# Two layers of attention and experts: first loads, first maxima, score order and expert weights moved

## The chip, the cores and the metric

The kernel runs on one core of a Trainium2 chip. The metric is the device time of one execution in microseconds (us). Three runs of the kernel before gave 2292.01, 2292.16 and 2296.86 us; the median is 2292.16 us.

## What is computed

Two transformer layers on x of shape (2, 1024, 128), all in float32, each with a layer norm ahead of it:

```python
x = x + _L0_attn_ref(_layernorm(x), ...)   # 16 heads of 8, rotary embedding, plain softmax attention
x = x + _L0_ffn_ref(_layernorm(x), ...)    # one shared and 7 routed experts of width 352, top 2, silu gate
x = x + _L1_attn_ref(_layernorm(x), ...)   # layer norm with gain, biases, plain attention, residual inside
x = x + _L1_ffn_ref(_layernorm(x), ...)    # below
```

The last of them has an attention with relative positions and 32 experts of width 128:

```python
q, k, v = x @ wq, x @ wk, x @ wv                        # 16 heads of 8
p = pe @ wp                                             # pe: sines and cosines of 2*1024-1 distances
ac = jnp.einsum('bihd,bjhd->bhij', q, k)
bd_full = jnp.einsum('bihd,phd->bhip', q, p)
bd = bd_full[:, :, jnp.arange(Ss)[:, None], rel]        # rel = i - j + Ss - 1
att = jax.nn.softmax((ac + bd) * scale, axis=-1)
src = src + attn_out @ wo
x2 = _layernorm(src, ln2_g, ln2_b)
sel = jax.nn.sigmoid(x2 @ sel_w)                        # top 4 of 32 kept as gate
h = jax.nn.relu(jnp.einsum('bsd,edh->bseh', x2, keys))
moe_out = jnp.einsum('bseh,ehd,bse->bsd', h, values, gate)
```

## The kernel before

The program is written for each engine by hand: every engine has its own list of steps, in the order of `plan`, and counts semaphores. The ten stages are `front(0)`, `attention(0)`, `front(1)`, `experts0`, `front(2)` (with the end of `experts0` ahead of it), `attention(1)`, `front(3)`, `relative_attention`, `front(4)`, `experts1`. The engines meet only after stages 3, 4, 9 and 10 (`MEETINGS`); elsewhere each runs on as far as its semaphores let it. In the profile, SP is the queue that issues every DMA, PE is TensorE, DVE VectorE, ACT ScalarE, POOL GpSimd.

**Fronts** (f = 0, 2, 3 lead to an attention). The tokens go through in four groups g of 512. For each group the layer norm is taken, transposed and multiplied with the weights; ACT rounds keys and queries to a high part (`projected`, lines 1293 to 1310, tile `hl`), DVE or POOL subtracts to get the low part, and SP stores both to `q_stack` and `k_stack` in DRAM (`q_out` line 322, `k_out` line 332: three DMAs of 256 KB each). There is one `hl`: ACT may write group g + 1 only when the stores of group g have landed (`stk_out`, `stq_out`). Groups 0 and 1 are batch 0, and so heads 0 to 15. In the third group (g = 2) SP waits for the stores of groups 0 and 1 and issues the loads of heads 0, 1 and 2 (`load_qk`, line 358: four DMAs of 128 KB for queries and four for keys of each head; `load_rel` adds one of 32 KB, line 363). In fronts 0 and 2 they stand between `q_out` and `k_out` of the third group, in front 3 behind both.

**Plain attention** (`attention`, stages 2 and 6, 32 heads each). The work of one head is a `position` with eight steps kt. In each step PE issues `turned` twice (T below, line 607: one matmul each, keys by queries turned, on rows 0 to 63 of the array, into banks 0, 1, 7), `scores` of the head two ahead (S below, line 587: two matmuls on rows 64 to 127, into banks 2, 3 or 4, 5) and `values` (line 617). DVE takes the maximum of each S (`row_max`, line 1114), ACT the exponential of each T (line 1373). T waits for an exponential that frees its bank, S for a maximum that frees its pair. The maxima go as a row into the head's queries (`max_row`, `max_copy`, `max_rows`), so T has the maximum subtracted. S of heads 0 and 1 are made ahead of the first position.

**Relative attention** (stage 8). The same scheme; a head's positions are prepared by four `prep` (PE line 676 into bank 7, DVE line 1130, POOL lines 1604 and 1606, ACT line 1402), and each S is two `stack_scores` (line 685) and two `scores` (line 693) into banks 2 and 3, one pair only:

```python
e.wait_ge(max_done, 2 + 8 * (HB + n) + qt)
```

so that each S waits for the maximum (DVE line 1135) of the S just before it. T uses banks 0, 1, 4 and 5 (`TURN`). The S of heads 0 and 1 are made ahead of the first position, in four halves of four rows, each half after two `prep`.

**Last experts** (`experts1`, stage 10). For each of 32 experts x and four groups tg: PE multiplies keys (three matmuls of split operands, into bank tg), DVE gates (lines 1226, 1228), ACT rounds high (line 1491), POOL (tg 0, 1; line 1668) or DVE (tg 2, 3; line 1214) subtracts, PE multiplies values. PE's order is keys(x, tg), then values of the group before. The weights of an expert are split too: ACT rounds them (line 1498), POOL subtracts (line 1662) into `wsp`, which has four slots; POOL does so behind its two subtractions of the expert before, and keys(x, 0) waits for it (`wsp_ok`).

## Time and profile before

| | |
|---|---|
| the three runs, median | 2292.16 us |
| the profiled execution, its own time | 2293.8 us |
| its span, first to last instruction | 2291.8 us |
| PE busy | 2071.1 us (90%) |
| DVE busy | 1418.5 us (62%) |
| ACT busy | 1191.4 us (52%) |
| POOL busy | 518.3 us (23%) |
| mean granted TensorE clock | 0.927 of 2.4 GHz |
| line 1114, maxima of the plain attentions | 512, mean 1220 ns |
| line 1373, their exponentials | 1024, mean 589 ns |
| line 1135, maxima of the relative attention | 256, mean 1225 ns |
| line 1668, POOL's subtractions in the last stage | 64, mean 1292 ns |

A span holds everything from the first to the last instruction of the profiled execution; the execution's own time is 2.0 us longer. Matmuls are pipelined and their ends are modelled, so PE's busy share says little alone. A timeline gives instructions in order of time with the idle time before them and what ended it; the windows view gives busy time, granted clock and DMA traffic in stretches. PEclk 0.5 is 1.2 GHz, 1.0 is 2.4 GHz.

### The profile page before, as it was taken

To read this page: it belongs to the slowest core of one execution; us is meant where nothing else is said; L and a number is where in the kernel's file an instruction comes from. 1 tells how busy PE (TensorE), PEld (TensorE's weight loads), DVE (VectorE), ACT (ScalarE), POOL (GpSimd) and SP (SyncE) were. 2 spreads that over 40 slices of the span, in tenths; PEclk is the share of its full clock that TensorE was granted. 3 is DMA by queue.
4 is the path that set the end of the run, shared out by engine and by line. 5 is a ranking of instruction groups with operands and counts; after the bars stand their busy time and mean duration, and the time that the engine had idled before them with its cause. 6 is when DMAs were issued, how large, how long until landed. Compare 5 with 4: busy or idle time off the path is not lost.

```text
span 2291.8 us, 42807 instructions
## 1 busy us (share of the span) xinstructions
PE 2071.1 (90%) x13696; PEld 1163.3 (51%) x13696; DVE 1418.5 (62%) x1857; ACT 1191.4 (52%) x2289; POOL 518.3 (23%) x497
## 2 busy tenths in 40 slices
PE   5799999689984999999559999999999999976998
PEld 2244444367762344444325555555555555544776
DVE  4799999456655999996644444444444444335666
ACT  1488888456651688888203444444444444433443
POOL 1000000258861000000121221122212221013554
PEclk8599999789996799999758999999999999988999
DMA  7444453222105344442440112111221112013554
GB/s 235 110 107 123 105 124 87 68 80 85 46 0 151 99 120 108 124 105 78 136 108 22 44 48 59 43 43 43 58 48 43 43 45 62 8 49 126 205 189 158
DMA packets 94607, 202.48 MB, mean 88 GB/s; under 512 B 20368, under 2 KB 53648, under 8 KB 89104
## 3 DMA queue, kind: packets, MB, share of 16 engines
q1 hardware_dynamic: 94544, 201.69, 31.3%
q8 instruction: 33, 0.54, 0.1%
q14 instruction: 30, 0.25, 0.0%
HBM read 166.62 MB, written 36.57 MB: 89 GB/s over the span
## 4 chain that ended last, share of the span: by engine, by line
PE 38%; issue 5%; POOL 3%; DVE 3%; DMA 1%; SPq 1%; ACT 0%; POOLq 0%; DVEq 0%; ACTq 0%
PE PS L708 15%; PE PS L693 8%; PE PS L718 6%; PE PS L702 5%; POOL BIG_r L1668 2%; PE PS L676 2%; POOL PR_r L1662 1%; PE PS L781 1%; DVE M L1135 1%; PE PS L685 1%; SPq L358 0%; DMA Ws_r<-w_stack 0%; PE PS L726 0%; DMA rope<-r_dram 0%; DVE rt L1130 0%
## 5 line engine op out<-in xcount | busy, mean ns | idle before, releaser
L1114 DVE TENSOR_REDUCE M<-PS 128x1 f32<-128x1024 f32 x512 | 606.3, 1220 | 75.5 <-PE PS L587 71.4
L1373 ACT ACTIVATE PR<-PS 128x512 f32<-128x512 f32 x1024 | 535.2, 589 | 127.4 <-PE PS L607 126.7
L1135 DVE TENSOR_REDUCE M<-PS 128x1 f32<-128x1024 f32 x256 | 313.5, 1225 | 438.0 <-PE PS L693 438.0
L1410 ACT ACTIVATE PR<-PS 128x512 f32<-128x512 f32 x512 | 305.1, 597 | 463.3 <-PE PS L708 456.7
L607 PE MATMUL PS<-Qs_r,Ks_r 32*128 32x512 f32 x1024 | 371.2, 507 | 1.8 <-ACT PR L1373 1.4
L617 PE MATMUL PS<-PR,Va 128*32 128x256 f32 x4096 | 322.0, 399 | 0.0
L587 PE MATMUL PS<-Ks_r,Qs_r 32*128 32x512 f32 x1024 | 269.4, 521 | 43.3 <-DVE hl L1036 17.3
L607 PEld LDWEIGHTS PS<-Qs_r,Ks_r 32*128 32x128 f32 x1024 | 152.5, 186 | 251.1 <-ACT PR L1373 177.8
L1540 POOL TENSOR_TENSOR Va<-Vt,nil 128x64 f32<-128x64 f32 x96 | 27.7, 292 | 759.5 <-PE PS L617 627.7
L1604 POOL TENSOR_TENSOR qk<-rt 128x512 f32<-128x512 f32 x64 | 81.9, 1280 | 381.2 <-DVE rt L1130 381.2
L718 PE MATMUL PS<-PR,Va 128*32 128x256 f32 x2048 | 163.6, 391 | 0.1
L708 PE MATMUL PS<-BIG_r,Eh 128*128 128x512 f32 x512 | 159.3, 392 | 0.0
L617 PEld LDWEIGHTS PS<-PR,Va 128*32 128x32 f32 x4096 | 88.8, 110 | 125.3 <-ACT PR L1373 70.1
L685 PE MATMUL PS<-Ks_r,Qs_r 32*128 32x512 f32 x512 | 133.0, 514 | 15.9 <-DVE M L1135 15.9
L1630 POOL TENSOR_TENSOR BIG_r<-BIG,BIG_r 128x512 fp32r<-128x512 f32 (+1 forms) x96 | 128.8, 1350 | 34.1 <-ACT BIG_r L1439 34.1
L587 PEld LDWEIGHTS PS<-Ks_r,Qs_r 32*128 32x128 f32 x1024 | 101.1, 191 | 60.3 <-DVE M L1114 23.1
L702 PE MATMUL PS<-Qs_r,Ks_r 32*128 32x512 f32 x512 | 128.6, 498 | 0.0
L1192 DVE TENSOR_TENSOR BIG<-PS,SRC 128x512 f32<-128x512 f32 (+1 forms) x96 | 66.1, 688 | 81.5 <-PE PS L781 78.7
L781 PE MATMUL PS<-BIG_r,PR_r 128*128 128x512 f32 x384 | 109.6, 395 | 4.8 <-POOL BIG_r L1668 4.8
L781 PE MATMUL PS<-Ah,PR_r 128*128 128x512 f32 x352 | 110.2, 394 | 0.0
L708 PEld LDWEIGHTS PS<-BIG_r,Eh 128*128 128x128 f32 x512 | 96.1, 188 | 21.5
L1668 POOL TENSOR_TENSOR BIG_r<-BIG,BIG_r 128x512 fp32r<-128x512 f32 x64 | 82.6, 1292 | 94.6 <-ACT BIG_r L1491 92.4
(174 smaller groups left out, 3035.8 us busy)
## 6 DMA issues: line engine op xcount, KB each, us to landing
Qs_r<-q_stack SPq DMA_DIRECT2D x384, 128.0 KB, 2.6
Ks_r<-k_stack SPq DMA_DIRECT2D x384, 128.0 KB, 3.1
Qs<-g_dram SPq DMA_DIRECT2D x30, 1024.0 KB, 4.9
o_dram<-Ob SPq DMA_DIRECT2D x96, 128.0 KB, 2.4
Ks<-g_dram SPq DMA_DIRECT2D x10, 1024.0 KB, 5.0
q_stack<-hl SPq DMA_DIRECT2D x36, 256.0 KB, 3.1
k_stack<-hl SPq DMA_DIRECT2D x36, 256.0 KB, 4.0
Ks<-in_kv SPq DMA_DIRECT2D x32, 128.0 KB, 2.0
```

The costliest lines, as they stand in the source:

```text
L587: m = e.matmul(bank(2 + 2 * (qt % 2) + kh), Qs_r[rows_, s, qt * P:(qt + 1) * P], Ks_r[rows_, s, kh * GW:(kh + 1) * GW], start=True, stop=True)
L607: e.matmul(bank(RING[(x if x < 4 else x + 1) % 3]), Ks_r[rows_, s, kt * P:(kt + 1) * P], Qs_r[rows_, s, qh * GW:(qh + 1) * GW], start=True ...
L617: m = e.matmul(PS[32 * g:32 * g + VC, 6, 0:256], Va[:, s, kt, :], PR[:, kt % 4, g * 256:(g + 1) * 256], start=(kt == 0), stop=(kt == QT - 1))
L693: m = e.matmul(bank(2 + kh), Ahs[s][:, qt * P:(qt + 1) * P], Eh[:, kh * GW:(kh + 1) * GW], start=False, stop=True)
L702: e.matmul(bank(TURN[kt % 2][qh]), Ks_r[rows_, s, kt * P:(kt + 1) * P], Qs_r[rows_, s, qh * GW:(qh + 1) * GW], start=True, stop=False)
L708: m = e.matmul(bank(TURN[kt % 2][qh]), e_part[:, kt * P:(kt + 1) * P], a_part[s][:, qh * GW:(qh + 1) * GW], start=False, stop=(k == 2))
L718: m = e.matmul(PS[32 * g:32 * g + VC, 6, 0:256], Va[:, s, kt, :], PR[:, kt % 4, g * 256:(g + 1) * 256], start=(kt == 0), stop=(kt == QT - 1))
L781: m = e.matmul(out, w[a], h[b], start=start and n == 0, stop=n == 2 or not start, skip_group_check=not start)
L1114: e.tensor_reduce(M[:, s, qt:qt + 1], PS[:, 2 + 2 * (qt % 2):4 + 2 * (qt % 2), :] .rearrange("p a b -> p (a b)"), AX.X, ALU.max, negate=Tr ...
L1135: e.tensor_reduce(M[:, s, qt:qt + 1], PS[:, 2:4, :].rearrange("p a b -> p (a b)"), AX.X, ALU.max, negate=True).then_inc(max_done, 1)
L1373: e.activation(PR[:, kt % 4, qh * GW:(qh + 1) * GW], bank(RING[(x if x < 4 else x + 1) % 3]), ACT.Exp, scale=SCALE).then_inc(exp_done, 1)
L1410: e.activation(PR[:, kt % 4, qh * GW:(qh + 1) * GW], bank(TURN[kt % 2][qh]), ACT.Exp)\
```

## The change

Four parts. (1) In the third group of fronts 0, 2 and 3, SP now first waits for the stores of groups 0 and 1 and issues head 0's loads, then `q_out` and `k_out`, then the loads of heads 1 and 2. (2) In the plain attentions each step's S is issued ahead of its two T. (3) In the relative attention, S of heads 0 and 1 take the bank pairs 2, 0 and 4 in turn, so each waits for the maximum three rows back; the first position waits for all sixteen maxima, because its T use banks 0, 1, 4 and 5. (4) In `experts1` ACT and POOL split the weights of expert x + 2 during expert x: ACT behind the high part of group 1, POOL behind the subtractions of expert x as before; those of experts 0 and 1 are split at the start.

```diff
+        FIRST = [2, 0, 4]
...
                     a = QKV.index(f)
-                    q_out(a, g)
-                    if f == 3:
-                        k_out(a, g)
                     if g == 2:
 
                         e.wait_ge(stq_out, 16 * TERMS * (4 * a + 2))
                         e.wait_ge(stk_out, 16 * TERMS * (4 * a + 2))
                         e.wait_ge(pad_in, 16 * 3)
-                        if f < 3:
-                            for n in range(3):
+                        if f == 3:
+                            e.wait_ge(w_out_ok, 16 * 6)
+                            load_rel(0, 0)
+                        else:
+                            load_qk(0, 0)
+                    q_out(a, g)
+                    k_out(a, g)
+                    if g == 2:
+                        for n in range(1, 3):
+                            if f == 3:
+                                load_rel(n, n)
+                            else:
                                 load_qk(n, n)
-                        else:
-                            e.wait_ge(w_out_ok, 16 * 6)
-                            for n in range(3):
-                                load_rel(n, n)
-                    if f < 3:
-                        k_out(a, g)
...
                     for kt in range(QT):
-                        turned(n, s, 2 * kt)
-                        turned(n, s, 2 * kt + 1)
                         if ahead:
                             if kt == 0:
                                 e.wait_ge(qk_in[s2], 128 * (NH // SLOTS * a + block + (s >= 2) + 1))
                             scores(n + 2, s2, kt)
+                        turned(n, s, 2 * kt)
+                        turned(n, s, 2 * kt + 1)
...
-                def stack_scores(n, s, qt):
-
-                    e.wait_ge(max_done, 2 + 8 * (HB + n) + qt)
+                def stack_scores(n, s, qt, bk=2):
+
+                    e.wait_ge(max_done, 2 + 8 * (HB + n) + qt - (2 if isinstance(n, int) and n < 2 else 0))
...
-                        e.matmul(bank(2 + kh), Qs_r[rows_, s, qt * P:(qt + 1) * P],
+                        e.matmul(bank(bk + kh), Qs_r[rows_, s, qt * P:(qt + 1) * P],
...
+                    if first:
+                        e.wait_ge(max_done, 2 + 8 * HB + 2 * QT)
...
-                            stack_scores(n, n, qt)
-                            scores(n, n, qt)
+                            stack_scores(n, n, qt, FIRST[(QT * n + qt) % 3])
+                            scores(n, n, qt, FIRST[(QT * n + qt) % 3])
...
-                            row_max(n, n, qt)
+                            row_max(n, n, qt, FIRST[(QT * n + qt) % 3])
...
-                    if tg == 0 and not (last and s == SLOTS - 1):
-                        weights(SLOTS * i + s + 1, (s + 1) % SLOTS, 2 * i + (s + 1) // 2)
+                    if tg == 1 and not (last and s >= SLOTS - 2):
+                        weights(SLOTS * i + s + 2, (s + 2) % SLOTS, 2 * i + (s + 2) // 2)
...
                     if not last:
-                        weights(x + 1, (s + 1) % SLOTS)
+                        weights(x + 2, (s + 2) % SLOTS)
```

How it moves instructions, at three places. First SP's queue in front 0, from the second group's stores to the end of the front, before:

```order
L322 DMA q_stack<-hl 16x8x512 x3
L332 DMA k_stack<-hl 16x8x512 x3
L322 DMA q_stack<-hl 16x8x512 x3
L358 DMA Qs_r<-q_stack 32x1024 x4
L358 DMA Ks_r<-k_stack 32x1024 x4
L358 DMA Qs_r<-q_stack 32x1024 x4
L358 DMA Ks_r<-k_stack 32x1024 x4
L358 DMA Qs_r<-q_stack 32x1024 x4
L358 DMA Ks_r<-k_stack 32x1024 x4
L332 DMA k_stack<-hl 16x8x512 x3
L322 DMA q_stack<-hl 16x8x512 x3
L332 DMA k_stack<-hl 16x8x512 x3
```

and after (lines of the new file are one higher there):

```order
L323 DMA q_stack<-hl 16x8x512 x3
L333 DMA k_stack<-hl 16x8x512 x3
L359 DMA Qs_r<-q_stack 32x1024 x4
L359 DMA Ks_r<-k_stack 32x1024 x4
L323 DMA q_stack<-hl 16x8x512 x3
L333 DMA k_stack<-hl 16x8x512 x3
L359 DMA Qs_r<-q_stack 32x1024 x4
L359 DMA Ks_r<-k_stack 32x1024 x4
L359 DMA Qs_r<-q_stack 32x1024 x4
L359 DMA Ks_r<-k_stack 32x1024 x4
L323 DMA q_stack<-hl 16x8x512 x3
L333 DMA k_stack<-hl 16x8x512 x3
```

The third group's key stores stand behind eight loads instead of twenty-four, its query stores behind eight instead of none.

Second, PE in the first position of the first plain attention, steps 0 and 1 (L607 is T, L587 S; values are not there yet), before:

```order
L607 MATMUL PS<-Qs_r,Ks_r 128x512 [waits exp_done,m_in0,mt_copied]
L607 MATMUL PS<-Qs_r,Ks_r 128x512 [waits exp_done]
L587 MATMUL PS<-Ks_r,Qs_r 128x512 [waits max_done,qk_in2]
L587 MATMUL PS<-Ks_r,Qs_r 128x512
L607 MATMUL PS<-Qs_r,Ks_r 128x512 [waits exp_done] x2
L587 MATMUL PS<-Ks_r,Qs_r 128x512 [waits max_done]
L587 MATMUL PS<-Ks_r,Qs_r 128x512
```

and after (L609 is T, L589 S):

```order
L589 MATMUL PS<-Ks_r,Qs_r 128x512 [waits qk_in2,max_done,m_in0,mt_copied]
L589 MATMUL PS<-Ks_r,Qs_r 128x512
L609 MATMUL PS<-Qs_r,Ks_r 128x512 [waits exp_done] x2
L589 MATMUL PS<-Ks_r,Qs_r 128x512 [waits max_done]
L589 MATMUL PS<-Ks_r,Qs_r 128x512
L609 MATMUL PS<-Qs_r,Ks_r 128x512 [waits exp_done] x2
```

S, with its wait for a maximum, is now ahead of the waits for exponentials, in every step.

Third, ACT at the start of the last stage (L1498 rounds an expert's weights, L1491 a group's gated keys), before:

```order
L1498 ACTIVATE PR_r<-Ks 128x2x128 [waits gt_ok_a,stage_dve,stage_pe,ew_in0,stage_pool,stage_sp]
L1491 ACTIVATE BIG_r<-BIG 128x512 [waits hf_ok]
L1498 ACTIVATE PR_r<-Ks 128x2x128 [waits ew_in1]
L1491 ACTIVATE BIG_r<-BIG 128x512 [waits hf_ok]
L1491 ACTIVATE BIG_r<-PS 128x512 [waits hf_ok] x2
```

and after (L1502 and L1495):

```order
L1502 ACTIVATE PR_r<-Ks 128x2x128 [waits gt_ok_a,stage_dve,stage_pe,ew_in0,stage_pool,stage_sp]
L1502 ACTIVATE PR_r<-Ks 128x2x128 [waits ew_in1]
L1495 ACTIVATE BIG_r<-BIG 128x512 [waits hf_ok] x2
L1502 ACTIVATE PR_r<-Ks 128x2x128 [waits ew_in0]
L1495 ACTIVATE BIG_r<-PS 128x512 [waits hf_ok] x2
```

Two experts' weights are rounded before the first gated keys, and the third's follow behind groups 0 and 1 of expert 0.

## Rows read from the trace of the kernel before

**Rows 1.** The page, part 2: granted TensorE clock, tenths, 40 equal slices

```profile
PEclk8599999789996799999758999999999999988999
```

**Rows 2.** Timeline of SP's queue, first front: start us, us, line, transfers, count

```profile
33.95 1.89 SPq L332 DMA_DIRECT2D k_stack<-hl  x3
...
42.48 1.84 SPq L322 DMA_DIRECT2D q_stack<-hl  x3
...
55.69 1.85 SPq L332 DMA_DIRECT2D k_stack<-hl  x3
```

**Rows 3.** Timeline of ACT, first front; in brackets idle before, and releaser

```profile
39.26 0.63 ACT L1293 ACTIVATE hl<-qk 128x512 fp32r<-128x512 f32 x1 [8.21 <-DMA k_stack<-hl]
...
62.98 0.63 ACT L1293 ACTIVATE hl<-PR 128x512 fp32r<-128x512 f32 x1 [21.60 <-DMA k_stack<-hl]
```

**Rows 4.** Timeline of ACT, front 2, ahead of the second attention

```profile
716.46 0.69 ACT L1301 ACTIVATE hl<-PS,cols 128x512 fp32r<-128x512 f32 x1 [1.59 <-DMA k_stack<-hl]
...
738.99 0.69 ACT L1301 ACTIVATE hl<-PS,cols 128x512 fp32r<-128x512 f32 x1 [20.41 <-DMA k_stack<-hl]
```

**Rows 5.** Timeline of ACT, then of PE, front 3, ahead of relative attention

```profile
1137.46 0.60 ACT L1303 ACTIVATE hl<-PS 128x512 fp32r<-128x512 f32 x1 [0.57 <-DMA k_stack<-hl]
...
1148.08 0.60 ACT L1303 ACTIVATE hl<-PS 128x512 fp32r<-128x512 f32 x1 [8.22 <-DMA k_stack<-hl]
...
1153.14 0.76 PE L676 MATMUL PS<-Qs_r,Ws_r 32*128 32x512 f32 x1 [8.71 <-DMA Ws_r<-w_stack]
```

**Rows 6.** Busy time by stretch: PE, PEld, DVE, ACT, POOL, PEclk, DMA share, GB/s

```profile
34.00:36.00 2.00, 2.00 (x6) 0.80 (x6) 1.40 (x3) 0.00 (x0) 0.00 (x0) 1.00 0.97 337
...
56.00:58.00 2.00, 0.00 (x0) 0.00 (x0) 0.00 (x0) 0.00 (x0) 0.00 (x0) 0.50 1.04 232
```

**Rows 7.** Timeline of PE, first relative scores: one row of maxima, next preparation

```profile
1168.86 0.79 PE L685 MATMUL PS<-Ks_r,Qs_r 32*128 32x512 f32 x2 [1.32 <-DVE M L1135]
...
1172.12 0.79 PE L685 MATMUL PS<-Ks_r,Qs_r 32*128 32x512 f32 x2 [1.32 <-DVE M L1135]
...
1173.99 0.79 PE L676 MATMUL PS<-Qs_r,Ws_r 32*128 32x512 f32 x1
...
1175.98 0.79 PE L685 MATMUL PS<-Ks_r,Qs_r 32*128 32x512 f32 x2
```

**Rows 8.** Busy time by stretch, start of the first plain attention

```profile
92.00:96.00 4.00, 4.00 (x32) 0.98 (x24) 2.97 (x3) 2.69 (x6) 0.00 (x0) 0.50 0.00 0
```

**Rows 9.** Timeline of PE's loads, one plain position; DVE, eight positions apart

```profile
245.20 0.18 PEld L607 LDWEIGHTS PS<-Qs_r,Ks_r 32*128 32x128 f32 x1 [0.23 <-ACT PR L1373]
...
245.29 0.19 PEld L587 LDWEIGHTS PS<-Ks_r,Qs_r 32*128 32x128 f32 x2
...
245.72 0.16 PEld L617 LDWEIGHTS PS<-PR,Va 128*32 128x32 f32 x8 [0.24 <-issue]
...
300.55 7.22 DVE L1114 TENSOR_REDUCE M<-PS 128x1 f32<-128x1024 f32 x6 [0.47 <-PE PS L587]
...
383.63 7.22 DVE L1114 TENSOR_REDUCE M<-PS 128x1 f32<-128x1024 f32 x6 [0.48 <-PE PS L587]
```

**Rows 10.** Timeline of PE and POOL, last stage: keys of experts 3, 17, 31

```profile
2107.42 0.50 PE L781 MATMUL PS<-Al,PR_r 128*128 128x512 f32 x1
...
2190.33 0.74 POOL L1662 TENSOR_TENSOR PR_r<-Ks,PR_r 128x256 fp32r<-128x256 f32 x1
...
2191.20 0.49 PE L781 MATMUL PS<-Al,PR_r 128*128 128x512 f32 x1 [0.27 <-POOL PR_r L1662]
...
2192.68 0.39 PE L781 MATMUL PS<-Al,PR_r 128*128 128x512 f32 x1
...
2194.05 0.39 PE L781 MATMUL PS<-Al,PR_r 128*128 128x512 f32 x1
...
2274.83 0.49 PE L781 MATMUL PS<-Al,PR_r 128*128 128x512 f32 x1 [0.20 <-POOL PR_r L1662]
```

**Rows 11.** Groups by line, last stage: count, busy us, mean ns, idle before, releaser

```profile
L1491 ACT ACTIVATE BIG_r<-BIG 128x512 fp32r<-128x512 f32 x64 | 40.4, 632 | 67.8 <-DVE BIG L1226 67.8
```

More of the change, by code:

```diff
@@ L678, in prep, with scores @@
                         .then_inc(prep_ps, 1)
-                def stack_scores(n, s, qt):
-                    e.wait_ge(max_done, 2 + 8 * (HB + n) + qt)
+                def stack_scores(n, s, qt, bk=2):
+                    e.wait_ge(max_done, 2 + 8 * (HB + n) + qt - (2 if isinstance(n, int) and n < 2 else 0))
                     for kh in range(2):
                         rows_ = slice((2 + kh) * KR, (3 + kh) * KR)
-                        e.matmul(bank(2 + kh), Qs_r[rows_, s, qt * P:(qt + 1) * P],
+                        e.matmul(bank(bk + kh), Qs_r[rows_, s, qt * P:(qt + 1) * P],
                                  Ks_r[rows_, s, kh * GW:(kh + 1) * GW], start=True, stop=False)
-                def scores(n, s, qt):
+                def scores(n, s, qt, bk=2):
                     if qt % 4 == 0:
@@ L692, in scores @@
                     for kh in range(2):
-                        m = e.matmul(bank(2 + kh), Ahs[s][:, qt * P:(qt + 1) * P], Eh[:, kh * GW:(kh + 1) * GW],
+                        m = e.matmul(bank(bk + kh), Ahs[s][:, qt * P:(qt + 1) * P], Eh[:, kh * GW:(kh + 1) * GW],
                                      start=False, stop=True)
@@ L1502, in unit @@
                     high(v, tg)
-                    if tg == 0 and not (last and s == SLOTS - 1):
-                        weights(SLOTS * i + s + 1, (s + 1) % SLOTS, 2 * i + (s + 1) // 2)
+                    if tg == 1 and not (last and s >= SLOTS - 2):
+                        weights(SLOTS * i + s + 2, (s + 2) % SLOTS, 2 * i + (s + 2) // 2)
                 weights(0, 0, 0)
+                weights(1, 1, 0)
                 for s in range(SLOTS):
@@ L1670, in expert @@
                     if not last:
-                        weights(x + 1, (s + 1) % SLOTS)
+                        weights(x + 2, (s + 2) % SLOTS)
                 weights(0, 0)
+                weights(1, 1)
                 with e.Fori(0, NE1 // SLOTS - 1) as i:
@@ L1677, in experts1 @@
                 for s in range(SLOTS):
-                    expert(NE1 - SLOTS + s, s, s == SLOTS - 1)
+                    expert(NE1 - SLOTS + s, s, s >= SLOTS - 2)
             plan = [lambda: front(0), lambda: attention(0), lambda: front(1), experts0, lambda: front(2),
```

6 lines of the change are left out of this document (3 added, 3 removed).

## The prediction

> **What bounds the kernel now.** I read the page first, for the clock [rows 1]: it dips at the fronts and at the two starts of attention, where PE waits for something else. Then the timelines of those starts, and one position of each loop. Four places matter.
>
> In fronts 0 and 2 the third group's key stores stand behind 24 loads of 128 KB. ACT waits 21.60 us for them in front 0 [rows 3] and 20.41 us in front 2 [rows 4], and with ACT the last group's queries and keys, and PE's first scores. SP's queue shows why: query stores at 42.48, key stores at 55.69 [rows 2]. Front 3 has a smaller wait, 8.22 us [rows 5], and there PE starts only when head 0's last load lands (8.71 us). At the start of relative attention each row of maxima takes 3.26 us (1168.86 to 1172.12), since PE and DVE take turns on one bank pair [rows 7]. In the plain attentions a position takes (383.63 - 300.55)/8 = 10.39 us, and DVE is idle 0.47 us in one of its two breaks [rows 9]. In the last stage an expert takes (2274.83 - 2107.42)/28 = 5.98 us, and each starts just behind POOL's weight subtraction [rows 10].
>
> **Part 1, loads.** SP now waits for the second group's stores, landed when ACT goes on at 39.26 [rows 3], then issues head 0's eight loads. Twenty-four took from 44.32 to 55.69, 0.47 us each [rows 2], so eight take 3.8: query stores are issued at 43.1 instead of 42.48, key stores at 45.0 instead of 55.69. In the second group key stores needed from 33.95 to 39.26, 5.3 us, with nothing ahead of them [rows 2, 3]; that gives 50.3. By bytes: 1.05 MB of loads at 232 GB/s is 4.5 us, 1.57 MB of stores at 337 GB/s 4.7 us [rows 6], so from 39.3 all is moved at 48.5, about the same with a landing. The last group's queries are ready near 50.3 anyway, so that is also the floor. I take 50.9 for 62.98: **12 us**. Moved behind the stores are heads 1 and 2, 2.1 MB or 9 us more: all in by about 60; PE starts near 53, head 1 is wanted eight maxima of 1.2 us later, at 62, head 2 at 71. The last group's stores and the first row of maxima queue behind those loads on SP until about 66, and position 0 wants that row at 71: covered, by little; if the cover is gone, 1 to 2 us come back.
>
> Front 2 is the same from 716.46 [rows 4]: loads to 720.3, key stores issued at 722.2, landed at 727.5 instead of 738.99: **11.5 us**. In front 3 the stores had nothing ahead of them, so now they get later: nine loads from 1137.46 take 4.3 us, key stores are issued at 1143.7 and land at 1149.0, against 1148.08 [rows 5]. But head 0's load is in by then, and PE has only to wait for the passes that follow on ACT (0.60) and DVE (two of 0.7), some 2 us: 1151.5 instead of 1153.14, **1.5 us**. Bounds: if head 0's bytes hold back the stores in full, 4.5 us less in each of the first two fronts and front 3 gains nothing, so 14.5; at the top 26. Sum taken: 25.
>
> **Part 3, bank pairs.** A row that waits for nothing takes PE from 1172.12 to 1173.99, 1.87 us at 1.2 GHz [rows 7]; the maximum (1.2 us) is hidden beside it. The step from a half's last row to the next half's first stays: DVE finishes the last maximum, multiplies, PE prepares once more (1172.12 to 1175.98, 3.86 us). So each half saves 3 x (3.26 - 1.87) = 4.17 us. In the last half position 0 now waits for all sixteen maxima, 3.3 us after the last row starts instead of 1.87; but its first score of head 2 stood at 3.26 before, so nothing more is lost. Behind that wait are only T and S of position 0. Four halves give 16.7; the transpose of head 0's maxima, which lay in a wait, now costs 0.6. **16 us**. POOL's two passes of 1.3 us and ACT's of 0.6 between them prepare a half in some 3.7 us and have over 9. Bounds: 12, if two of three rows still wait in part; at the top the clock rival below.
>
> **Part 4, expert weights.** In steady state one group's keys and values take 2192.68 to 2194.05, 1.37 us, four of them 5.46, against 5.98: 0.52 us x 28 = 14.6 [rows 10]. Expert 1 and expert 3 add 0.9. The wait is POOL's: its subtraction (0.74 us behind two of 1.29) ends at 2191.07 and keys start at 2191.20. With the weights split one expert earlier nothing on POOL stands before keys. What is late next: the path from keys to values of group 0 runs over DVE's gating, about as long as ACT's rounding, 0.63 us [rows 11], and POOL's 1.29, 2.6 us with little between; values of group 0 come six blocks of 0.68 us after the keys' end, 4.1. DVE has six passes of 0.7, 4.2 us in 5.46. Neither binds. No DMA is added, and the weights' loads get earlier. **15.5 us**; bounds 10 (a new wait of 0.2 us an expert) and 16.
>
> **Part 2, scores first.** PE is in order, and a step ends with values, which start 0.43 us after the last T or S. Where the second T waits for an exponential, S comes 0.09 us after it (245.20, 245.29, values 245.72) [rows 9]. With S gone ahead values come 0.09 sooner; four steps in eight are like this, 0.36 us a position at best. Against it, T starts behind two score loads where all four are ready: 0.09 us by the same rows, in three places on the chain through ACT, 0.27. DVE is fed earlier, but its eight maxima, 7.22/6 us each, fill only 9.6 us of the position; the chain is T to exponential to T. Between 0.36 gained and 0.36 lost (half of a 0.18 us load at each of four steps) I take 0.13 gained, for 60 positions **8 us**; bounds -22 and +22.
>
> The Trainium skill, TensorEngine Tiling, Key Properties, says that different tiles of the array load weights and multiply in parallel; by that T would lose nothing to S and this part would give 0.27 us or more a position, 16 us, and the whole 2219. No row here has S ahead of T, so it isn't shown.
>
> **Sum.** 25 + 16 + 15.5 + 8 = 64.5 us. The profiled execution took 2293.8 us around a span of 2291.8; so 2229.3. The median shown is 1.6 us lower than that execution: **2227.5 us**.
>
> **Rivals.** (a) *The clock rises inside the first relative scores.* A row at 1.2 GHz takes 1.87 us; at 2.4 DVE's 1.2 would bound it. The gaps in which PE idled are mostly gone. Three halves of four at the higher clock give 3 x 4 x 0.65 = 8 us more: 2219.5. Against: PE was busy all through 92 to 96 us, in the first position, and stayed at 0.50 [rows 8]. Chance 0.2. The Trainium skill, TensorE: Matmul & The Clock Gate, Part 1, says that sustained matmul activity releases the throttle; by it this rival would be the forecast. The row just named speaks against it as a certainty.
>
> (b) *S first gives nothing.* T's delay eats what values gain, or more: +5 us for part 2 instead of -8: 2240. For it: the exponentials, not the maxima, end PE's waits in the loop. Chance 0.14.
>
> (c) *Stores still queue behind head 0*, part 1 at 14.5: 2238. Chance 0.1.
>
> (d) *Slower.* In every step S's two weight loads, 0.18 us, go ahead of T with nothing beside them, and every one lies on the chain of exponentials: 8 x 0.18 = 1.44 us a position, 60 positions 86 us, against 56.5 from the others: +30, 2322. It decides from 0.94 us a position on. Against: S's two loads start 0.09 us after T's today, and take 0.19 together with values 0.43 behind [rows 9]. Chance 0.03.
>
> (e) *The new order does not do what it says*, because the first fronts' stores or maxima run into the later loads, and each start loses 6 us again while the rest holds: 2245. Chance 0.05.
>
> **Numbers.** The forecast, with its own spread of some 8 us, has 0.48. Rival (a) takes the range down to 2210, (b), (c) and (e) up to 2246; that leaves out (d) and tails, under 2 in 10. A measurement of this kernel can tell some 0.2%, 4.6 us, from no change. Every case but (d) is faster by more: faster 0.95, same 0.02, slower 0.03.
>
> **What would show it.** ACT's wait for `k_stack` in fronts 0 and 2 falls from over 20 us to under 10, and PE's first scores come near 53 and, counted from front 2's third group, 11 to 12 us sooner. In the first relative scores PE's stacks stand 1.9 us apart within a half, and the wait of line 685 for DVE is gone. Experts come 5.46 us apart, and no wait for POOL's weight subtraction is left. Plain positions take near 10.25 us. It would be wrong if positions take over 10.4, if the store waits only move to the last group, or if experts stay above 5.8.

## The result, and the profile after

The changed kernel takes 2222.36 us, median of 4 runs (2216.49 to 2225.35); the kernel before, run beside it, 2292.09. The ratio is 0.9681, with a 95% interval of 0.9661 to 0.9702, so it is some 73 us faster (68 to 78); the two medians differ by 69.7. The forecast was 2227.5 us, with a range of 2210 to 2246. The profiled execution took 2220.77 us around a span of 2218.8, against a span of 2291.8: 73.0 us less.

The first question is where these 73.0 us lie. The table cuts both spans at marks that stand in the timelines: the starts of DVE's first, 16th and 32nd maximum of an attention, and the end of ACT's last exponential of it. Microseconds, one profiled execution each; "p1" to "p4" are the four parts of the change alone, in the experiments below.

| stage | before | after | p1 | p2 | p3 | p4 |
|---|---|---|---|---|---|---|
| start to attention 0's first maximum | 65.6 | 54.1 | 52.9 | 65.1 | 65.2 | 66.2 |
| its first 32 maxima | 43.6 | 40.4 | 39.6 | 43.9 | 38.4 | 44.0 |
| from there to its last exponential | 310.7 | 305.5 | 310.6 | 305.7 | 310.6 | 314.3 |
| to attention 1's first maximum | 322.1 | 311.8 | 309.7 | 321.7 | 322.2 | 323.3 |
| its first 32 maxima | 38.9 | 38.7 | 43.6 | 41.9 | 38.9 | 38.7 |
| from there to its last exponential | 314.0 | 305.4 | 310.8 | 305.5 | 313.8 | 314.0 |
| to the first relative maximum | 69.3 | 68.1 | 67.8 | 68.6 | 69.2 | 69.6 |
| to the 16th relative maximum | 50.7 | 34.6 | 50.7 | 50.7 | 34.6 | 50.7 |
| to the last relative exponential | 818.5 | 817.8 | 818.5 | 817.7 | 817.9 | 817.9 |
| from there to the end | 258.3 | 242.5 | 257.7 | 258.4 | 258.2 | 240.7 |

Part 1 is the first, fourth and seventh line: 11.5, 10.3 and 1.2 us, 23.0 together. Part 3 is the eighth, 16.1, and part 4 the last, 15.8. The attentions' lines hold 17.2 us, of which part 2 is only some; the rest is the clock, as shown below.

**Fronts.** ACT in the changed kernel, the second and third group's keys of front 0, then of fronts 2 and 3:

```profile
40.11 0.63 ACT L1297 ACTIVATE hl<-qk 128x512 fp32r<-128x512 f32 x1 [8.40 <-DMA k_stack<-hl]
51.40 0.63 ACT L1297 ACTIVATE hl<-PR 128x512 fp32r<-128x512 f32 x1 [9.17 <-DMA k_stack<-hl]
...
697.91 0.69 ACT L1305 ACTIVATE hl<-PS,cols 128x512 fp32r<-128x512 f32 x1 [1.48 <-DMA k_stack<-hl]
708.72 0.69 ACT L1305 ACTIVATE hl<-PS,cols 128x512 fp32r<-128x512 f32 x1 [8.87 <-DMA k_stack<-hl]
...
1098.18 0.60 ACT L1307 ACTIVATE hl<-PS 128x512 fp32r<-128x512 f32 x1 [0.99 <-DMA k_stack<-hl]
1110.68 0.60 ACT L1307 ACTIVATE hl<-PS 128x512 fp32r<-128x512 f32 x1 [10.26 <-DMA k_stack<-hl]
```

The waits of 21.60 and 20.41 us [rows 3, 4] are 9.17 and 8.87. The two groups stand 11.29 us apart in front 0 instead of 23.72, 10.81 instead of 22.53 in front 2. In front 3 it goes the other way, as forecast: 12.50 apart instead of 10.62 [rows 5], because nine loads now stand ahead of the stores. SP's queue in front 0, transfers in the last column:

```profile
40.10 1.74 SPq L359 DMA_DIRECT2D Qs_r<-q_stack  x4
...
43.74 1.85 SPq L323 DMA_DIRECT2D q_stack<-hl  x3
45.64 2.34 SPq L333 DMA_DIRECT2D k_stack<-hl  x3
```

Key stores leave at 45.64 instead of 55.69 [rows 2]; the forecast had 45.0. PE's first scores of attention 0 and its first preparation in front 3:

```profile
53.24 1.22 PE L589 MATMUL PS<-Ks_r,Qs_r 32*128 32x512 f32 x4 [6.36 <-DVEq L1114]
...
1112.73 0.79 PE L678 MATMUL PS<-Qs_r,Ws_r 32*128 32x512 f32 x1 [6.77 <-DVE hl L1042]
```

PE starts at 53.24 (forecast: near 53). In front 3 the wait for a load of `Ws_r`, 8.71 us [rows 5], has become one of 6.77 for DVE's last subtraction (the low part of the last group's queries).

**First relative scores.** PE, one half of head 0 and then the start of position 0:

```profile
1121.95 0.80 PE L687 MATMUL PS<-Ks_r,Qs_r 32*128 32x512 f32 x2
...
1123.83 0.79 PE L687 MATMUL PS<-Ks_r,Qs_r 32*128 32x512 f32 x2
...
1125.70 0.79 PE L687 MATMUL PS<-Ks_r,Qs_r 32*128 32x512 f32 x2
...
1159.80 0.79 PE L704 MATMUL PS<-Qs_r,Ks_r 32*128 32x512 f32 x2 [1.32 <-DVE M L1139]
```

Rows stand 1.88 and 1.87 us apart, with no wait for DVE within a half, where they stood 3.26 apart [rows 7]. The new wait for all sixteen maxima is the 1.32 us in front of line 704.

**Last stage.** POOL, from one expert to the next:

```profile
2111.84 2.65 POOL L1673 TENSOR_TENSOR BIG_r<-BIG,BIG_r 128x512 fp32r<-128x512 f32 x2 [2.10 <-ACT BIG_r L1495]
...
2117.28 2.65 POOL L1673 TENSOR_TENSOR BIG_r<-BIG,BIG_r 128x512 fp32r<-128x512 f32 x2 [2.10 <-ACT BIG_r L1495]
```

Experts are 2117.28 - 2111.84 = 5.44 us apart, against 5.98 [rows 10]. POOL now waits 2.10 us in each, and no instruction of the stage waits for line 1667, its weight subtraction, where PE waited 30 times before.

**Plain positions.** DVE, one position apart, then PE's weight loads: step 0, in which the second T waits, and from steps 2 and 3 the first loads and the values (steps count from 0, as `kt` does).

```profile
243.72 5.80 DVE L1118 TENSOR_REDUCE M<-PS 128x1 f32<-128x1024 f32 x5 [0.54 <-PE PS L589]
...
253.90 1.22 DVE L1118 TENSOR_REDUCE M<-PS 128x1 f32<-128x1024 f32 x1 [0.53 <-PE PS L589]
```

```profile
247.76 0.18 PEld L589 LDWEIGHTS PS<-Ks_r,Qs_r 32*128 32x128 f32 x2 [0.41 <-issue]
247.78 0.18 PEld L609 LDWEIGHTS PS<-Qs_r,Ks_r 32*128 32x128 f32 x1
248.27 0.18 PEld L609 LDWEIGHTS PS<-Qs_r,Ks_r 32*128 32x128 f32 x1 [0.31 <-ACT PR L1377]
248.69 0.16 PEld L619 LDWEIGHTS PS<-PR,Va 128*32 128x32 f32 x8 [0.24 <-issue]
...
250.46 0.19 PEld L589 LDWEIGHTS PS<-Ks_r,Qs_r 32*128 32x128 f32 x2 [0.22 <-issue]
250.56 0.18 PEld L609 LDWEIGHTS PS<-Qs_r,Ks_r 32*128 32x128 f32 x1
...
252.35 0.59 PEld L619 LDWEIGHTS PS<-PR,Va 128*32 128x32 f32 x16 [0.24 <-ACT PR L1377]
```

A position takes 253.90 - 243.72 = 10.18 us, not 10.39 [rows 9]. Where T waits for an exponential, values start 0.42 us behind it (248.27 to 248.69); with S in between it was 0.52 (245.20 to 245.72) [rows 9]. T's first load starts 0.02 us behind S's in step 0, and 0.10 in step 2, where the step before ended with the transposition of maxima; 1.89 us pass from there (250.46) to the values of step 3 (252.35).

**The clock.** In tenths, 40 equal slices of the changed kernel's span:

```profile
PEclk8799999699996899999759999999999999986999
```

Two pairs of stretches of 10 us, first of the changed kernel and then of the one before (columns: PE, PEld, DVE, ACT and POOL busy with counts, PEclk, DMA share, GB/s):

```profile
90.00:100.00 10.00, 10.00 (x102) 4.05 (x98) 9.35 (x9) 8.51 (x18) 0.29 (x1) 1.00 0.46 126
...
1040.00:1050.00 10.00, 9.60 (x81) 3.66 (x81) 0.00 (x0) 8.83 (x19) 0.00 (x0) 1.00 0.07 21
```

```profile
90.00:100.00 10.00, 10.00 (x71) 3.24 (x70) 6.90 (x6) 6.20 (x12) 0.00 (x0) 0.50 0.37 91
...
1080.00:1090.00 10.00, 9.59 (x70) 3.39 (x62) 0.00 (x0) 7.30 (x15) 0.00 (x0) 0.76 0.25 78
```

In the kernel before, PE is still granted 0.50 (1.2 GHz) at 90 to 100 us, behind a start at 65, and it falls from full clock again at 1080 to 1090 us, inside attention 1's last positions, which end at 1095. In the changed kernel the higher level (2.4 GHz) is there from 85 us on, behind a start at 53, and it lasts over the end of attention 1. These are most of the 3.2 us in the table's second line (some 0.5 of it is part 2's) and 3.3 of the 8.6 in the sixth (the same loop took 310.7 us in attention 0 and 314.0 in attention 1 before; after, 305.5 and 305.4).

The rise is not tied to the change. Part 3 leaves the first attention alone, and its start was as late as before (65.2 us), yet in its execution the same stretch is at the higher level:

```profile
90.00:100.00 10.00, 9.97 (x99) 4.21 (x98) 9.07 (x9) 8.46 (x19) 0.29 (x1) 1.00 0.42 120
```

Its first 32 maxima took 38.4 us, where the kernel before, at 0.50 in this stretch, took 43.6.

### The profile page after: what moved, and what is told of

Same layout as the page of the kernel before. It is cut to its first block, busy times and chain, and to the rows that moved or that the text cites. A ratio compares the mean times of both kernels' runs of the same rounds, so it can differ in the third digit from the quotient of the medians.

```text
span 2218.8 us, 42827 instructions
## 1 busy us (share of the span) xinstructions
PE 2042.4 (92%) x13696; PEld 1148.4 (52%) x13696; DVE 1410.8 (64%) x1857; ACT 1190.7 (54%) x2289; POOL 518.4 (23%) x497
## 4 chain that ended last, share of the span: by engine, by line
PE 46%; DVE 2%; SPq 1%; issue 1%; DMA 1%; POOL 0%; ACT 0%; DVEq 0%; POOLq 0%; ACTq 0%
PE PS L710 16%; PE PS L695 8%; PE PS L785 8%; PE PS L720 6%; PE PS L704 5%; PE PS L678 2%; PE PS L687 0%; SPq L359 0%; DMA k_stack<-hl 0%; PE PS L728 0%; DMA rope<-r_dram 0%; PE PS L524 0%; DVE rt L1134 0%; PE PS L545 0%; SPq L323 0%
## 5 line engine op out<-in xcount | busy, mean ns | idle before, releaser
L609 PE MATMUL PS<-Qs_r,Ks_r 32*128 32x512 f32 x1024 | 378.1, 503 | 1.2 <-ACT PR L1377 0.9
L589 PE MATMUL PS<-Ks_r,Qs_r 32*128 32x512 f32 x1024 | 268.2, 519 | 22.4 <-DVE M L1118 11.0
L589 PEld LDWEIGHTS PS<-Ks_r,Qs_r 32*128 32x128 f32 x1024 | 99.6, 191 | 201.9 <-issue 133.7
L609 PEld LDWEIGHTS PS<-Qs_r,Ks_r 32*128 32x128 f32 x1024 | 152.9, 184 | 89.9 <-ACT PR L1377 64.7
L704 PE MATMUL PS<-Qs_r,Ks_r 32*128 32x512 f32 x512 | 128.4, 498 | 1.3 <-DVE M L1139 1.3
L695 PE MATMUL PS<-Eh,Ah 128*128 128x512 f32 x256 | 102.0, 483 | 0.0
```

Source lines behind the costliest of these rows:

```text
L589: m = e.matmul(bank(2 + 2 * (qt % 2) + kh), Qs_r[rows_, s, qt * P:(qt + 1) * P], Ks_r[rows_, s, kh * GW:(kh + 1) * GW], start=True, stop=True)
L609: e.matmul(bank(RING[(x if x < 4 else x + 1) % 3]), Ks_r[rows_, s, kt * P:(kt + 1) * P], Qs_r[rows_, s, qh * GW:(qh + 1) * GW], start=True ...
L695: m = e.matmul(bank(bk + kh), Ahs[s][:, qt * P:(qt + 1) * P], Eh[:, kh * GW:(kh + 1) * GW], start=False, stop=True)
L704: e.matmul(bank(TURN[kt % 2][qh]), Ks_r[rows_, s, kt * P:(kt + 1) * P], Qs_r[rows_, s, qh * GW:(qh + 1) * GW], start=True, stop=False)
```

## The experiments

All comparisons are with runs of the kernel before on the same chip.

### The four parts alone

Each is the kernel before with one part of the diff. Their expectations, on record before they ran:

> The kernel before with part 1 alone (head 0's loads ahead of the third group's stores, the other two heads' behind them, in fronts 0, 2 and 3). Theory F (the forecast's terms): 25 us less than before, near 2267; ACT's wait for k_stack in fronts 0 and 2 falls from 21.6 and 20.4 us to 8 to 10, plain positions stay at 10.39 us. Theory G (the 8.5 us that the whole change gained over the forecast lie in part 1): 30 us or more less, from two things that the trace after shows beside the forecast's terms: the clock rises near 85 us instead of 105 in the first attention (3 to 4 us), and front 3 to the first relative maximum takes 88.5 us instead of 93.1 (3 us more than the forecast's 1.5). If the later loads ran into the first positions, under 20.

> The kernel before with part 2 alone (S ahead of the two T in each step of the plain positions). Theory F: 8 us less, positions at 10.25. Theory T (T starts with S in another part of the array and loses nothing to it): 0.20 us a position, as in the trace after, 12 us in 60 positions, 2280; PE's loads for T start 0.01 to 0.02 us behind those of S. Theory C (the shorter position of the trace after needs the earlier clock or the other parts): positions at 10.35 or more and under 3 us less.

> The kernel before with part 3 alone (three bank pairs for the first two heads' relative scores). Theory F: 16 us less, 2276; rows 1.87 us apart. Rival: with the gaps gone from before's own front 3 the clock rises within the first rows, then 20 us or more; a rival below: under 12, if the position that waits for all sixteen maxima gives part back.

> The kernel before with part 4 alone (expert weights two ahead). Theory F: 15.5 us less, 2276.5; experts 5.46 us apart. Theory P (PE alone bounds an expert now, 12 products of 0.227 us in each of two halves of four blocks): 5.44, 15.8 us less with the 2 us of the first experts. Rival: 5.6 or more, 10 us less or under, if a wait for DVE's gating or ACT's rounding takes the place of POOL's.

The kernel before had a median of 2294.93 us here (11 runs).

| part | median us | ratio, 95% interval | less than before | its own stages in the table |
|---|---|---|---|---|
| 1, loads | 2268.28 | 0.9884 [0.9867, 0.9901] | 26.6 [22.7, 30.5] | 12.7 + 12.4 + 1.5 = 26.6 |
| 2, S first | 2281.40 | 0.9929 [0.9914, 0.9945] | 16.3 [12.6, 19.7] | 5.0 + 8.5 = 13.5 |
| 3, bank pairs | 2274.62 | 0.9913 [0.9898, 0.9927] | 20.0 [16.8, 23.4] | 16.1 |
| 4, weights | 2273.65 | 0.9902 [0.9887, 0.9918] | 22.5 [18.8, 25.9] | 17.6 |

By stages each part does alone what it does in the whole: ACT's wait for `k_stack` is 9.01 us in front 0 and 9.39 in front 2 with part 1, positions take 10.18 us with part 2 and stay at 10.39 with part 1, rows stand 1.87 us apart with part 3, experts 5.44 with part 4. So theory F holds for part 1, T for part 2 (C falls: it needs neither the earlier clock nor another part), F for part 3, P for part 4 (F's 5.46 us an expert and P's 5.44 are hardly apart). For part 2, 3.3 of the 8.5 us in attention 1 are the clock, as above, which leaves 10.2. G falls by the stages: part 1's own hold 26.6 us, and the 3 us more that G looked for in front 3 lie ahead of front 3, in attention 1's last positions. The total doesn't settle it, its interval ends at 30.5. The earlier clock that G named did come in part 1's execution (first 32 maxima 39.6 us), but it came in part 3's too.

The ratios of the four multiply to 0.963, 84 us, where the whole measures 73. The parts' own stages don't have this surplus: they add to 26.6 + 13.5 + 16.1 + 17.6 = 73.8 us, the whole's 73.0 within 1. The kernel before is in all four ratios, and its median in these runs, 2294.93 us, is 2.7 to 3.5 above those of the other comparisons here (2292.09, 2292.21, 2291.40); counted four times that is 11 us or more. Against 2292.2 the four medians are 71 us less together. So the surplus is most likely the comparison's and not the parts'; the parts were not run again to show it. The table shows another scatter: the first 32 maxima of an attention take between 38.4 and 44.0 us with identical code there (p3, p4 and the kernel before in attention 0), and the rest of an attention 310.6 to 314.3. Both follow the clock. A single execution is thus worth a few us either way, and a part of under 5 us can't be read from its total, only from its stage.

### S between the two T

```
                        turned(n, s, 2 * kt)
                        if ahead:
...
                            scores(n + 2, s2, kt)
                        turned(n, s, 2 * kt + 1)
```

> The changed kernel with S between the two T of each plain step (T, S, T) instead of ahead of both. Theory V (part 2's gain is that values no longer start behind an S that follows T's wait for an exponential: in the trace after, values start 0.42 us behind the second T where it waits, 0.52 before): the same time as the changed kernel within 2 us, positions 10.18, since the last of a step is T here too. Theory D (the gain comes from DVE's maxima being fed earlier, since all S stand first): positions between 10.25 and 10.39, 4 to 12 us slower than the changed kernel.

2212.33 us, ratio 0.9650 [0.9630, 0.9670], and 10.05 us a position, better than both kernels. Neither theory had this: V had 10.18, D over 10.25. The attentions' stages from the 32nd maximum on are 301.8 and 301.7 us against 305.5 and 305.4. PE's weight loads in steps 2 and 3 of a position:

```profile
248.09 0.18 PEld L609 LDWEIGHTS PS<-Qs_r,Ks_r 32*128 32x128 f32 x1 [0.28 <-ACT PR L1377]
248.17 0.19 PEld L589 LDWEIGHTS PS<-Ks_r,Qs_r 32*128 32x128 f32 x2
248.57 0.18 PEld L609 LDWEIGHTS PS<-Qs_r,Ks_r 32*128 32x128 f32 x1 [0.22 <-ACT PR L1377]
...
249.45 0.18 PEld L609 LDWEIGHTS PS<-Qs_r,Ks_r 32*128 32x128 f32 x1 [0.21 <-ACT PR L1377]
249.87 0.59 PEld L619 LDWEIGHTS PS<-PR,Va 128*32 128x32 f32 x16 [0.24 <-ACT PR L1377]
```

From the first T to values it is 249.87 - 248.09 = 1.78 us, where S first takes 1.89 from S to values. Here each of the four T waits for ACT, so S in front of the first one shows: steps 2 and 3 are 0.10 us shorter together, in the mean of 46 positions. The other steps differ by 0.06 us at most, some one way and some the other, and by 0.03 in sum.

### Half maxima: is DVE's wait the reason?

```
-  PS[:, 2 + 2 * (qt % 2):4 + 2 * (qt % 2), :].rearrange("p a b -> p (a b)")
+  PS[:, 2 + 2 * (qt % 2), :]
```

> The changed kernel (S, T, T in each plain step) with the maxima of the plain attentions taken over the first 512 of the 1024 scores only; the other half of the maximum is left out, so DVE has about 0.7 us instead of 1.22 for each row. Together with the next kernel. Theory W (with S first, T stands behind S's wait for DVE's maximum; PE was idle 63 us for it in the changed kernel, 24 us with S between the two T): without that wait the two orders take the same, within 0.03 us a position, both at 9.9 to 10.05. Theory X (the 0.13 us between the two orders comes from how the loads of S and T follow each other on PE): the two stay 0.10 or more apart, this one near 10.15.

> The kernel with S between the two T (10.05 us a position) with the same half maxima. Theory W: within 0.03 us a position of the kernel with S first and half maxima, 9.9 to 10.05. Theory X: 9.9 to 10.05 here and 10.10 or more there. If positions fall well below 9.9 in both, DVE's eight maxima (9.8 us) bounded the position with S between, and not ACT.

Both kernels leave out the second half of each maximum. The totals are 2211.76 and 2202.23 us (2 runs each); they gain at the starts, where the first 16 maxima take 11.9 us instead of 17.0. DVE in the steady loop, the same maximum one position apart, first with S first and then with S between:

```profile
246.64 0.69 DVE L1118 TENSOR_REDUCE M<-PS 128x1 f32<-128x512 f32 x1 [1.53 <-PE PS L589]
...
256.82 0.69 DVE L1118 TENSOR_REDUCE M<-PS 128x1 f32<-128x512 f32 x1 [1.53 <-PE PS L589]
```

```profile
244.44 0.69 DVE L1118 TENSOR_REDUCE M<-PS 128x1 f32<-128x512 f32 x1 [1.16 <-PE PS L589]
...
254.50 0.69 DVE L1118 TENSOR_REDUCE M<-PS 128x1 f32<-128x512 f32 x1 [1.17 <-PE PS L589]
```

10.18 and 10.06 us: exactly the positions with full maxima. W falls, X holds; and DVE bounds neither order, though it is busy 36.79 of 40 us with full maxima. The 62.8 us for which the trace after has the loads of S wait for DVE's maxima cost nothing in the loop, only at the starts.

### Values in pairs, plain and relative

```
                        if kt >= 3 and kt % 2 == 1:
                            values(n, s, kt - 3)
                            values(n, s, kt - 2)
```

> The changed kernel with the values of two steps together in every second step of the plain positions (steps 1, 3, 5, 7), in place of one in nearly every step; nothing else moves. In the trace after, PE's weight loads stop 0.41 us at each turn from values to scores and 0.24 us at each turn from scores to values, and two values in a row take 1.00 us against 0.57 each plus the turns. Theory B (these turns between two shapes of weights bound PE, and PE bounds the position): three turns of each kind fewer, PE's share of a position falls by up to 1.3 us, and the position falls from 10.18 to what DVE's eight maxima allow, 9.8 to 9.9: 17 to 23 us faster. Theory E (the chain T, exponential, T bounds it and the turns lie beside it): 10.1 to 10.3, within 6 us of the changed kernel. Rival on the other side: steps without values come too fast for ACT and steps with two too late, over 10.3, 8 us or more slower.

2308.20 us, ratio 1.0056 [1.0032, 1.0079]: 86 us more than the changed kernel, and 0.6% above the kernel before. Its 12 runs spread from 2296.54 to 2333.72 us, wider than those of any other kernel here, and the profiled one took 2326.03. Positions take 11.12 us. PE in the loop, and a stretch of 40 us:

```profile
245.19 0.50 PE L609 MATMUL PS<-Qs_r,Ks_r 32*128 32x512 f32 x1 [0.51 <-ACT PR L1377]
245.62 1.07 PE L619 MATMUL PS<-PR,Va 128*32 128x256 f32 x16
...
247.93 0.49 PE L609 MATMUL PS<-Qs_r,Ks_r 32*128 32x512 f32 x1 [0.50 <-ACT PR L1377]
```

```profile
200.00:240.00 40.00, 32.93 (x350) 15.40 (x349) 34.14 (x30) 31.64 (x65) 0.89 (x3) 1.00 0.38 100
```

The rival on the other side came true. PE is busy 32.93 of 40 us, 9.2 of the 11.12 us of a position: it did become free, and now waits 0.5 us for an exponential in every second step. The reading is that with values gone from between them the T come as fast as three banks allow, and that behind the pair ACT has run dry. So DVE doesn't bound the position, and PE's own work, in this order, doesn't either; what is left is the chain T, exponential, T, which only an even spread of values keeps going. That chain is read from the waits: no kernel shortened the exponential or gave T a fourth bank, which would have tested it. Attention 1 suffered more: five of its positions in a row took 17.15 us, at a granted clock of 0.50.

In relative attention ACT has time to spare, so the same edit was tried there, on the kernel with S between:

```
                        elif kt % 2 == 0:
                            values(n, s, kt - 2)
                            values(n, s, kt - 1)
```

> The kernel with S between the two T, and in relative attention the values of two steps together in every second step (steps 0, 2, 4, 6). Theory B2 (each turn between two shapes of weights costs PE 0.2 to 0.4 us, and here PE alone bounds the step, ACT having 450 us idle): every second turn from products to values and from values to scores goes, 0.25 to 0.4 us in each of 124 pairs of steps, positions from 25.85 to 24.3 to 24.9 and 30 to 50 us less than the kernel with S between. Theory E2 (what sank the pairs in the plain positions holds here too, the chain from T over the exponential to T binds): positions at 25.9 or more, the same or slower. Between: the turn is only moved (from products straight to scores costs about as much as over values), within 0.1 us a position.

2217.71 us, ratio 0.9671 [0.9650, 0.9692]; positions 25.87 us instead of 25.85. It gains nothing. PE's weight loads around a pair of values and around a step without them:

```profile
1506.53 0.19 PEld L710 LDWEIGHTS PS<-Ah,Eh 128*128 128x128 f32 x1
...
1507.08 0.59 PEld L720 LDWEIGHTS PS<-PR,Va 128*32 128x32 f32 x16 [0.36 <-issue]
1508.08 0.18 PEld L704 LDWEIGHTS PS<-Qs_r,Ks_r 32*128 32x128 f32 x2 [0.41 <-ACT PR L1417]
...
1517.04 0.19 PEld L710 LDWEIGHTS PS<-Ah,Eh 128*128 128x128 f32 x1
1517.59 0.18 PEld L704 LDWEIGHTS PS<-Qs_r,Ks_r 32*128 32x128 f32 x2 [0.36 <-issue]
```

A pair of values takes 1.00 us from its first load to the next scores, a single one 0.57, so a second one costs 0.43: the 0.41 us in which the weight loads stop behind values are nearly all the values' own columns passing through, and the turn is 0.57 - 0.43 = 0.14. Without values, products to scores take 0.55 us, as much as products to values. Of the 0.25 to 0.4 us that B2 had per pair of steps 0.12 can be had (two times 1.11 against 1.55 + 0.55), 0.48 in the four pairs of a position, and even these don't show; where they go wasn't settled.

### Where the loads and the banks have to be

Head 0's loads too behind the third group's stores, in all three fronts:

```
                         if f == 3:
                             e.wait_ge(w_out_ok, 16 * 6)
-                            load_rel(0, 0)
-                        else:
-                            load_qk(0, 0)
                     q_out(a, g)
                     k_out(a, g)
                     if g == 2:
-                        for n in range(1, 3):
+                        for n in range(3):
```

> The changed kernel with head 0's loads too behind the third group's stores (query stores, key stores, then all three heads' loads). Theory K (what pays in fronts 0 and 2 is that the key stores leave the queue ahead of 16 or more loads; where head 0's stand is worth little, since the last group's key stores and passes take until the start anyway): ACT's wait for k_stack falls from 9.2 to 5 or 6 us, head 0's loads land about when PE is ready, and the time is within 3 us of the changed kernel, up to 4 us faster. Theory H (head 0 ahead is needed): PE waits for head 0's last load, its first scores come later than 53.2 us, and front 3 goes back to its wait for Ws_r (8.7 us before): 3 to 8 us slower.

2224.24 us, ratio 0.9716 [0.9693, 0.9739], within the 3 us of K. ACT and PE in front 0:

```profile
50.21 0.63 ACT L1294 ACTIVATE hl<-PR 128x512 fp32r<-128x512 f32 x1 [8.70 <-DMA k_stack<-hl]
```

```profile
55.27 1.22 PE L586 MATMUL PS<-Ks_r,Qs_r 32*128 32x512 f32 x4 [7.56 <-DMA Ks_r<-k_stack]
```

ACT's wait is 8.70 us and not the 5 or 6 that K had. POOL, SP and DVE in the same front show why:

```profile
41.32 1.27 POOL L1571 TENSOR_TENSOR hl<-qk,hl 128x512 fp32r<-128x512 f32 x1
42.68 1.84 SPq L323 DMA_DIRECT2D q_stack<-hl  x3
44.56 1.90 SPq L333 DMA_DIRECT2D k_stack<-hl  x3
46.56 0.69 DVE L1008 TENSOR_TENSOR PR<-rt 128x512 f32<-128x512 f32 x1
48.61 0.69 DVE L1015 TENSOR_TENSOR qk<-rt 128x512 f32<-128x512 f32 x1
```

The query stores can't leave before POOL's subtraction ends, at 42.59, so with no loads ahead of them the key stores leave at 44.56, only 1.08 us sooner than in the changed kernel: most of head 0's eight loads (40.10 to 43.70 there) stand in a gap in which SP has nothing else to issue. From there to ACT it is 5.65 us, against 5.76.

PE waits for head 0's last load (H), and in front 3 for a load of `Ws_r` again, 7.33 us. The stage marks put the starts 2.0 us later in front 0, 0.2 sooner in front 2 and 0.6 later in front 3, but in this execution the code ahead of the third groups ran 0.7 us quicker in front 0 and some 2 in the stages up to front 2. Counted from the third group's first key rounding, PE starts after 15.88 us in front 0 (55.27 - 39.39) for 13.13 in the changed kernel, 15.03 for 12.99 in front 2 and 15.20 for 14.55 in front 3: 5.4 us later in all. So of part 1's 25 us, counted in the same way, some 20 come from key stores ahead of sixteen or more loads, and 5 from head 0 going first. The totals can't tell: 1.9 us between the medians, with intervals that overlap.

Two bank pairs in place of three, and no wait of position 0:

```
-        FIRST = [2, 0, 4]
+        FIRST = [2, 4]
-                    if first:
-                        e.wait_ge(max_done, 2 + 8 * HB + 2 * QT)
```

> The changed kernel with two bank pairs (2 and 3, 4 and 5) in place of three for the first relative scores, each row behind the maximum two rows back, and without position 0's wait for all sixteen maxima, since its first T writes neither pair. Theory Q (a maximum of 1.22 us fits into a row of 1.87 us of PE, so one row of slack is enough): rows 1.87 us apart as with three, the time equal within 1.5 us, position 0's first T up to 1.3 us earlier. Rival: a row waits 0.1 to 0.4 us for the maximum two rows back, 1 to 5 us slower.

```profile
1163.88 0.79 PE L704 MATMUL PS<-Qs_r,Ks_r 32*128 32x512 f32 x2
1165.26 0.79 PE L687 MATMUL PS<-Ks_r,Qs_r 32*128 32x512 f32 x2 [0.59 <-DVE M L1137]
```

Sixteen maxima take 34.6 us as with three pairs (Q), and position 0's first T stands right behind the last row; but the 0.59 us wait is now S's, and S starts 2.54 us behind the last row's products (1162.72), where it was 2.55 (1157.26 to 1159.81). The third pair gains nothing, and the wait costs nothing. The total is 2227.31 us, ratio 0.9722 [0.9699, 0.9745], 5 us higher than the changed kernel's; in its profiled execution the first 32 maxima of the attentions, in which nothing was changed, took 44.0 and 43.7 us against 40.4 and 38.7, 8.6 more, and the rest 5.3 less.

Last, S between and two pairs together:

> The changed kernel with S between the two T in the plain positions and two bank pairs, without position 0's wait, in the first relative scores: the version that the runs so far point to. By the stages measured so far (positions 10.05 instead of 10.18, first relative rows 34.6 us for sixteen maxima with two pairs as with three) 2212 us, 2206 to 2218 with the spread of the starts; 8 to 10 us under the changed kernel. If the 10.05 us does not repeat, or if the 2227 us with two pairs came from the pairs and not from the starts' clock, 2218 to 2222.

2213.51 us, ratio 0.9655 [0.9634, 0.9676], positions of 10.05 us. The gain of S between repeats; the version is as fast as with three pairs and simpler. Against the changed kernel's 0.9681 [0.9661, 0.9702] the intervals overlap, but the stages (301.9 and 301.7 us for 305.5 and 305.4) don't leave the 7 us to the clock.

## Why the prediction was right

**Part 1, 25 us forecast, 23.0 in the whole and 26.6 alone.** Right step by step: key stores at 45.6 for 45.0, ACT at 51.4 for 50.9, PE at 53.2 for 53, and in front 3 the stores later and the start earlier. Counted from the third group's keys, as the forecast did, front 0 gave 12.4 us for 12 (23.72 to 11.29), front 2 11.7 for 11.5 (22.53 to 10.81) and front 3 1.1 for 1.5 (15.68 to 14.55 until PE's start): 25.3. The 23.0 of the table is less because in this execution the code ahead of the third groups took 0.9 us longer in the first line and 1.4 in the fourth.

One step of it was not so. The forecast took 50.3 us, when the last group's queries were ready, for a floor. In the kernel with head 0's loads behind the stores that group's keys were ready at 47.25 and its queries at 49.30, and ACT still waited until 50.21, for the stores. The landing of the key stores sets the start, and the floor is lower than the forecast had it. Nothing came back through SP's queue: the row of maxima left at 65.05 and position 0 was not held.

**Part 3, 16 us forecast, 16.1 measured,** with the row of 1.87 us. Rival (a), the clock rising inside these scores, did not happen in any run: the sixteen maxima took 34.6 us in all ten kernels that had two or three pairs.

**Part 4, 15.5 us forecast, 15.8 in the whole, 17.6 alone.** An expert takes 5.44 us for 5.46. The stage takes between 240.6 and 243.1 us in all ten kernels with this part, and the clock divides them: in the five that take 242.4 us or more the lower level lasts 3.4 us longer early in the stage.

**Part 2, 8 us forecast, about 11 measured** (10.18 us a position for the 10.25 forecast; 5.2 us in attention 0 and 8.6 - 3.3 in attention 1 from the 32nd maximum on, and some 0.5 before it). The way was right, the sizes were not, and the 0.13 us a position is not what its two terms give, 0.36 - 0.27 = 0.09.

The loss was too large: "T starts behind two score loads where all four are ready: 0.09 us by the same rows, in three places on the chain through ACT, 0.27". It measures 0.01 to 0.02 us where S and T follow values, and 0.10 only in step 2, behind the transposition. The 0.09 was read from rows in which S stood behind T's wait; where nothing waited, the kernel before already had its loads 0.01 us apart (242.44 and 242.45).

The gain was too large as well: 0.09 us in each of four steps. Values do start 0.10 us sooner behind a T that waits, but that T now starts later in its step: 0.30 us behind the step's first load instead of 0.26 in steps 5 and 7, and 0.50 instead of 0.41 in step 0. In the mean of 46 positions of each kernel steps 5 and 7 became 0.05 us shorter each, and step 0 0.07. Step 1 became 0.05 shorter, since what follows the transposition is S and no longer a T that waits. Steps 2 and 3 together became 0.01 longer, and the other two are the same: 0.20 us in all. Two wrong sizes partly made up for each other, so that the 8 us come near the 11 is in part luck.

The Trainium skill, TensorEngine Tiling, Key Properties, says that different tiles load and multiply in parallel, and by that this part was to give 16 us. The 0.01 to 0.02 us agree with the rule. The part gave less because only about half of the gain stayed in each step, and because of the 0.10 us in step 2.

**What the sum lacked, some 6 us.** The forecast held the clock's rise and fall fixed in both attentions. In the profiled execution the higher level came at 85 us behind a start at 53, where it had come at 105 behind a start at 65, and it did not end before attention 1 did. As far as the runs show, this is luck and no gain of the change: with the same code in the attention its first 32 maxima take 38.4 us (p3), 43.6 (before) or 44.0 (p4), and the rest of attention 1 310.8 (p1), 313.8 (p3) or 314.0 (before and p4). Of the 8.5 us between the sum of 64.5 and the 73.0 measured, about 2.7 and 3.3 are the clock, 3 part 2, 0.7 the relative loop (818.5 to 817.8, the scatter of the same code), 0.4 parts 3 and 4, and part 1 takes 2 off. What sets the moment at which the clock rises was not tried.

## What to carry to other kernels

Read a stage's gain from the stage, not from the total: here four parts agree with their rows within 3 us each once the clock's share is taken off, while totals scatter by 5 through the clock at the starts. A baseline that stands in several comparisons carries its own scatter into each. A PE that hardly idles, a DVE at 92% and an ACT at 85% (36.79 and 33.90 of 40 us) can all be beside the bound when, as the waits here suggest, a short ring of banks ties T to the exponential three back: then what stands between the T sets the time, and taking PE's work out of one step and into the next made the position 9% longer. In such a loop put work that depends on nothing between the two links that wait, neither ahead of both nor behind both, and move stores that the next stage's producer waits for ahead of loads that nobody needs yet.

## What the runs showed of the hardware

Loads of S and T in different parts of the array start 0.01 to 0.02 us apart when both follow values, and 0.10 apart behind the transposition (250.46 and 250.56). The idle time of PE's weight loads behind values (0.41 us) is nearly all the values' own streaming, shown by doubling them (0.57 and 1.00 us). With the values in pairs the same loop ran at the higher clock level in attention 0 and at the lower for five positions and more in attention 1; the runs don't say why.
